# An attention and gated-MLP block on one core: the loop over four heads' units replaced by straight code with constants

## The reference

```python
mod = (silu(c) @ wmod).reshape(2, 6, 1, 256)           # sa, ca, ga, sb, cb, gb
ga, gb = sign(ga) * max(|ga|, 0.25), sign(gb) * max(|gb|, 0.25)
h = layernorm(x) * (1 + ca) + sa
q, k, v = h @ Wq + bq, h @ Wk + bk, h @ Wv + bv        # 16 heads of 128
q, k = rotary(q * 128 ** -0.5), rotary(k)
attn = softmax(causal(q @ k.T))                        # 1024 x 1024 for each head and batch
x = x + ga * (attn @ v @ Wo + bo)
h = layernorm(x) * (1 + cb) + sb
x = x + gb * down(silu(gate(h)) * up(h))               # int weights (w - 128) * scale, 704 hidden
```

## Time and profile before

| | before |
|---|---|
| median of 3 runs | 970.95 us |
| the profiled execution's own time | 968.9 us |
| its span | 967.0 us |
| PE busy | 934.2 us (97%), 5667 matmuls |
| DVE, ACT, POOL busy | 735.9, 673.4, 774.9 us |
| TensorE's granted clock, mean | 0.995 of full speed |
| instructions' own loading (queues q8 and q14) | 94 packets, 0.91 MB |

### The profile page before, as it was taken

How to read it: one execution, slowest core, us unless ns; L and a number is a source line. 1 busy time by engine, 2 the same in 40 slices (tenths; PEclk the granted TensorE clock), 3 DMA queues, 4 the chain that set the end, 5 groups by cost and what they waited for, 6 DMA issues and landing times.

```text
span 967.0 us, 20178 instructions
## 1 busy us (share of the span) xinstructions
PE 934.2 (97%) x5667; PEld 833.6 (86%) x5667; DVE 735.9 (76%) x1582; ACT 673.4 (70%) x1354; POOL 774.9 (80%) x555
## 2 busy tenths in 40 slices
PE   6989999999999999999999999999999999878898
PEld 5878998888889989989998888889989989767787
DVE  6766877778878877787877877887878777867544
ACT  5766766677677767676767677777777676757763
POOL 2468988898898988898889888998889888795653
PEclk9999999999999999999999999999999999999999
DMA  7554554554445545554455554644555545531011
GB/s 256 163 137 137 179 166 142 159 182 154 140 136 175 167 136 158 179 167 150 145 156 174 169 150 133 183 148 139 156 170 168 158 147 171 177 95 44 1 44 46
DMA packets 108978, 141.63 MB, mean 146 GB/s; under 512 B 12948, under 2 KB 80084, under 8 KB 108884
## 3 DMA queue, kind: packets, MB, share of 16 engines
q1 hardware_dynamic: 108884, 140.72, 48.5%
HBM read 62.36 MB, written 44.76 MB: 111 GB/s over the span
## 4 chain that ended last, share of the span: by engine, by line
PE 87%; DVE 3%; POOL 3%; issue 2%; ACT 2%; DMA 1%; SPq 0%; POOLq 0%; DVEq 0%; ACTq 0%
PE ps_r L1565 18%; PE ps_r L1564 18%; PE ps_r L1563 18%; PE ps_s L1563 7%; PE ps_s L1565 7%; PE ps_s L1564 7%; PE ps_t L1728 5%; PE ps_s L1570 1%; PE ps_s L1573 1%; PE ps_r L1570 1%; PE ps_r L1572 1%; PE ps_r L1668 1%; ACT probs L1046 1%; POOL pT_lo L782 1%; DMA wmod_a<-in_L_wmod 1%
## 5 line engine op out<-in xcount | busy, mean ns | idle before, releaser
L1046 ACT ACTIVATE probs<-ps_s,neg_max 128x128 f32<-128x128 f32 (+7 forms) x256 | 189.8, 742 | 84.5 <-DVE neg_max L1451 82.3
L764 POOL TENSOR_TENSOR swapped<-swapped,sin_sb 128x512 f32<-128x512 f32 x124 | 161.2, 1300 | 94.4 <-DMA swapped<-straight 94.1
L1451 DVE CUSTOM_DVE_ANT_0 ps_s<-ps_s,mask_wide 128x128 f32<-128x128 f32 (+7 forms) x256 | 193.6, 756 | 14.8 <-PE ps_s L1565 12.4
L782 POOL TENSOR_TENSOR pT_lo<-side_p,pT_hi 128x1024 fp32r<-128x1024 f32 (+2 forms) x93 | 195.3, 2131 | 0.7 <-ACT pT_hi L1035 0.7
L773 POOL TENSOR_TENSOR qk_lo<-swapped,qk_hi 128x512 fp32r<-128x512 f32 x124 | 159.4, 1297 | 19.7 <-ACT qk_hi L930 19.6
L767 POOL TENSOR_TENSOR swapped<-swapped,qk_cos 128x512 f32<-128x512 f32 x124 | 161.3, 1301 | 10.5
L1563 PE MATMUL ps_s<-qk_hi 128*128 128x512 f32 (+4 forms) x384 | 142.1, 370 | 2.4 <-ACT probs L1046 2.3
L1379 DVE STREAM_TRANSPOSE squares<-probs 128x1024 f32<-128x1024 f32 (+2 forms) x93 | 103.1, 1109 | 51.6 <-ACT probs L1046 48.4
L1565 PE MATMUL ps_r<-pT_hi,v_lo 128*128 128x512 f32 (+3 forms) x384 | 133.0, 346 | 0.0
L1564 PE MATMUL ps_r<-pT_lo,v_hi 128*128 128x512 f32 (+3 forms) x384 | 132.6, 345 | 0.0
L1565 PE MATMUL ps_s<-qk_hi,qk_lo 128*128 128x512 f32 (+4 forms) x384 | 131.4, 342 | 0.0
(11 more groups left out here) (205 smaller groups left out, 2409.3 us busy)
## 6 DMA issues: line engine op xcount, KB each, us to landing
swapped<-straight SPq DMA_DIRECT2D x252, 128.0 KB, 2.7
side_out<-squares SPq DMA_DIRECT2D x31, 512.0 KB, 2.6
side_p<-side_out SPq DMA_DIRECT2D x124, 128.0 KB, 2.9
side_out<-squares SPq DMA_DIRECT2D x31, 448.0 KB, 2.6
side_p<-side_out SPq DMA_DIRECT2D x124, 112.0 KB, 2.6
side_out<-squares SPq DMA_DIRECT2D x31, 384.0 KB, 2.3
side_p<-side_out SPq DMA_DIRECT2D x124, 96.0 KB, 2.2
x_in<-in_L_attn_x SPq DMA_DIRECT2D x4, 512.0 KB, 5.6
```

The costliest lines, as they stand in the source:

```text
L764: pool.tensor_tensor(swapped[:, q, :], swapped[:, q, :], sin_sb[:, at_], ALU.mult).then_inc(rotated, 1)
L782: pool.tensor_tensor(turned_at(t, 0, t + 1)(pT_lo).rearrange("p k (i c) -> p k i c", c=SQUARE), from_squares(side_p[t], t)[:, t::-1, :, :] ...
L1046: nc.scalar.activation(halved(t, probs[:, P_AT[step] * P:(P_AT[step] + t + 1) * P]), score_rows(step, t), ACT.Exp, bias=neg_max[:, t:t + 1 ...
L1451: nc.vector.tensor_tensor_reduce(rows, rows, halved(t, mask_wide[:, SEQ - n_keys:SEQ]), -1.0, -MASKED, ALU.add, ALU.min, accum_out=neg_max ...
```

## The change

On all five engines the loop is replaced by the same code written out for units 1 to 28, with `i` None, so that every wait and every address is a constant and there is no branch. The same edit stands five times, with the engine's name; PE's and SP's are:

```diff
-            with sp.Fori(0, LAST) as i:
-                run(Span(1, 1 + UNITS, i))
-            run(Span(ALL_UNITS - 3, ALL_UNITS + 1))
+            run(Span(1, ALL_UNITS + 1))
...
             pe.wait_ge(hT_ready, GROUPS4)
-            with pe.Fori(0, LAST) as i:
-                run(Span(1, 1 + UNITS, i))
-            run(Span(1 + LAST * UNITS, ALL_UNITS))
+            run(Span(1, ALL_UNITS))
```

More of the change, by code:

```diff
@@ L810, in _ @@
             run(Span(0, 1))
-            with pool.Fori(0, LAST) as i:
-                run(Span(1, 1 + UNITS, i))
-            run(Span(1 + LAST * UNITS, ALL_UNITS + 1))
+            run(Span(1, ALL_UNITS + 1))
             def gate_rows(n):
@@ L1158, in _ @@
             run(Span(0, 1))
-            with act.Fori(0, LAST) as i:
-                run(Span(1, 1 + UNITS, i))
-            run(Span(1 + LAST * UNITS, ALL_UNITS + 1))
+            run(Span(1, ALL_UNITS + 1))
             for n in range(HM, NCH * HM):
@@ L1523, in _ @@
             run(Span(0, 1))
-            with dve.Fori(0, LAST) as i:
-                run(Span(1, 1 + UNITS, i))
-            run(Span(1 + LAST * UNITS, ALL_UNITS + 1))
+            run(Span(1, ALL_UNITS + 1))
             def finish(first, size, src):
```

## The result

| | before | after |
|---|---|---|
| median | 970.62 us (14 runs, 969.86 to 973.19) | 972.35 us (14 runs, 971.46 to 973.45) |
| ratio of after to before, 95% interval | | 1.0018 (1.0010 to 1.0026) |
| the profiled execution, its span | 968.9, 967.0 us | 971.5, 969.6 us |
| units 2 to 28 (27 periods) | 699.31 us, 25.90 each | 701.10 us |
| packets of code on q8, on q14 | 17, 77 | 48, 45 |

The 14 runs of before include the three of which 970.95 us was the median, and eleven more, so the median differs a little. The change is slower. The amount, 1.7 us, lies just under the 0.2% that the prediction took as the limit of what can be told, and 14 runs a side do tell it: the interval excludes 1.

A forecast was written before the change was run, and what follows sets the result against it. The prediction took PE's unbroken matmuls in units 2 to 29 as the bound, with chains through other engines at start and ending. 968.9 less 0.15 gave 968.75; with the median 2.05 above that execution, 970.8 us, range 969.0 to 972.6.

The forecast's parts named there:

- What it adds: Loading of PE's written-out code, some 31 packets more on q8: taken as 0, at most 0.16 us.
- The slower rival: PE waits for its own code at 31 new packet boundaries: 4 us in all, time 975; chance 0.07.
- Point 3: Register instructions ahead of waits, about 40 ns each on DVE: removing them is worth 0.
- Point 1: PE's loop branch, met seven times, 208 to 238 ns where it goes back: hidden, removing it is worth 0.
- Point 2: Code loading after other engines' branches: DVE loses 0.88 us at a loop-back, ACT nothing; removing it is worth 0.
- The faster rival: DVE's stall at each loop-back is on the path: 6 times 0.88 us go, to 965.7; chance 0.05.
- Point 4: Register instructions in DVE's chain to `y` in unit 1: PE starts 0.15 us sooner, bounds 0 and 1.1.
- The ending: After the loop: PE's jump over the If's second arm, 3.41 us, stays under the last output's DMA with 2.7 us to spare.
- The sum: Whole kernel: 968.9 us of the profiled execution less 0.15 is 968.75; forecast for the median 970.8 us.
- no difference: Whole kernel: the time stays within 0.2%, 1.9 us, of the kernel before; chance 0.88.

The follow-up runs named there:

- e9: The kernel before, unchanged, measured once more against itself: 971.06 us, ratio 1.0000 (0.9991-1.0009).
- e8: The changed kernel with PE's loop put back and POOL's two waits in the other order: 970.72 us, ratio 0.9997 to the kernel before.
- e1: The changed kernel with POOL's two waits ahead of its addition in the other order: 971.30 us, ratio 1.0008 to the kernel before.

## Why the prediction was wrong

**The step that failed is "What it adds".** It said that 31 more loads of PE's code cost 0, at most 0.16 us. PE's program written out, alone, costs 1.0017 (1.0008 to 1.0026), some 1.6 us. The count was right (48 packets on q8, 17 before). Wrong was what was looked at: whether PE would wait for its code. It doesn't. The price is paid by SP's swap DMAs, 0.57 us on average for each that meets a load. It reaches PE by two ways: through POOL, DVE's `w_lo` and `v_lo`, or through ACT's `straight` and DVE's `qk_cos`. Where ACT keeps its loop there is a third, through ACT's branch and `o_lo`. The Trainium skill's page "Runtime: NRT & Kernel Launch", section "Instruction fetch mechanics", says that crossing from one block of code into the next is mostly hidden. That holds for the engine that fetches, in these rows, and not for the transfers beside it.

The bound of 0.16 us came from a single execution whose first round, with four loads, took 103.60 us. Another execution of the same kernel lost 1.06 us in that round (e9). Whether a load meets a swap at a bad place varies from one execution to the next; in the changed kernel six units of 27 lost something. One trace with four loads bounds the mean of 31 badly.

**The slower rival** had the right part of the program and a wrong mechanism. It set the point of decision at 0.06 us a load, and 1.83 us by 31 is 0.06; that is chance, since PE never waited for its code. Its argument against itself was that no period had grown, which is the same single trace.

**Point 3, register instructions ahead of waits: worth 0.** As a gain this was right, since no unit is shorter than 25.90 us. As an account of the change it missed that for two waits on one instruction the register form was the quicker one, 78 ns against 143. That could be read in the trace of before: POOL's units that are written out there already have 143 or 144 ns, 12 of the 124. It was not looked for, since POOL was not thought to bound anything.

**Point 1, PE's branch: worth 0.** Right. e8, in which PE alone has a loop, runs at 25.90 us a unit.

**Point 2, DVE's and ACT's code after a branch: worth 0.** Right as to the time, and as to DVE; wrong as to ACT. DVE's transpose of tile 6 in units 8 and 9 answers to the earlier trace rows:

```profile
263.66 1.11 DVE L1373 STREAM_TRANSPOSE squares<-probs 128x896 f32<-128x896 f32 x1 [1.17 <-ACT probs L1042]
...
289.55 1.11 DVE L1373 STREAM_TRANSPOSE squares<-probs 128x896 f32<-128x896 f32 x1 [1.17 <-ACT probs L1042]
```

It starts 14.54 and 14.52 us into the unit, so the stall of 0.88 us is gone, and no unit became shorter for it. The faster rival falls with that. Of ACT the prediction said that it loses nothing, since it is idle 2.84 us before `o_hi` in units 8 and 9 alike. In unit 9 most of that idle time is the delay behind its branch, 3.23 us from the branch at 14.40 us into the unit to the next instruction at 17.64, and PE's result at 17.87 hid it with 0.23 us to spare. In the eight traces with ACT's loop PE lost 0.07 to 0.54 us at 7 of 48 such places, 2.03 us in all or 0.25 a trace; in neither trace of the kernel before did it lose any. The six traces with ACT written out lost 0.05 us at most in these units. So unrolling ACT gives a margin back, which the kernel before did not need in its own two traces.

**Point 4, the chain in unit 1: 0.15 us.** Right as to the wait, which fell by 0.20 us, from 1.06 to 0.86, and it is 0.8 to 0.9 in all five experiments in which DVE is written out, against 1.0 to 1.1 in those in which it is not. The time it should have given is not seen, as unit 2 did not start sooner.

**The ending: unchanged.** Right as to PE's jump, still 3.56 us and under the output's DMA. What the ending took more is that DMA's own landing.

**The sum.** 970.8 us was forecast and 972.35 measured; the range to 972.6 held it, by the allowance for one load that shows on PE, which was made for another reason. The chance of 0.88 for "no difference" was too high: the claim rested on a row of matmuls without a break, and the prediction asked only what could delay PE itself, not how deep the cover of DVE's pieces was (some 0.35 us at `v_lo`).

## What to carry to other kernels

When a change makes an engine load code throughout, look at what its loads lie next to, and not only at whether that engine waits: here PE, which fetched, was never late for want of code, and the small DMAs of another engine were. A row of matmuls without a break in one trace says nothing on how near the next wait is; read, for every piece that PE takes from another engine, when it was ready and when it was needed, and take the smallest. Where a loop is to be unrolled, try it engine by engine: by the ratios all of the cost was in one program; the others' shortened a wait of the start by 0.2 us, and ACT's took away a delay that PE met now and then.

## What the runs showed of the hardware beside that

Two waits on one instruction of POOL, both against constants: the one that is written second goes to an instruction of its own, and if it is the one that comes last, the engine starts 65 ns later (143 against 78 ns, 124 of 124 cases, and 78 again with the order changed).

DVE's split with two inputs in SBUF, started while POOL works on SBUF, ended 0.54 to 0.55 us after POOL's instruction in 86 of 88 cases; in the two others it took 0.68 us.

TensorE's granted clock fell between 871 and 890 us in ten of the fourteen traces, those of before and after not among them. The stretch from 868 to 892 us of e1, in the columns of the earlier trace rows:

```profile
868.00:892.00 24.00, 18.82 (x98) 16.99 (x98) 18.51 (x60) 12.70 (x27) 10.19 (x14) 0.79 0.14 45
```

In the kernel before:

```profile
868.00:892.00 24.00, 17.61 (x118) 15.47 (x119) 17.59 (x58) 16.15 (x32) 11.96 (x11) 1.00 0.14 45
```

By the rows TensorE was at 2.4 GHz for all of these 24 us in the kernel before, and at 1.2 GHz for some 10 of them in e1 (0.21 by 0.5). Ahead of the fall it had been busy almost without a break to 851 us; in the stretch itself it is idle for a quarter of the time in either. From unit 31's first matmul to the end it takes 117.8 to 118.4 us in the four traces without such a fall, 118.7 to 118.9 in the three where it lasts 3.4 us, and 118.8 to 120.2 in the seven where it lasts 6.8 us or more. Together with losses in units 2 to 4 as in e9 this is of the size by which the first profiled execution lay under its kernel's median, 1.7 to 2 us; that these two make up that distance is not shown.
